# Two-layer graph network on one Trainium2 core: the first weight load in two parts, and the rounding of the first folded weight on two engines

## What is computed

```
# layer 0, seen as 2 batches of 4096 nodes in the shapes, computed per graph
q, k = split(x @ Wqk); v = x @ Wv
w    = (1/16) * mask * rowsum(q * (adj @ (k * mask)))
x1   = layernorm(x + softmax(w over the nodes) * v)
# layer 1
query, key, value = x1 @ Wq.T + bq, x1 @ Wk.T + bk, x1 @ Wv.T + bv
weight = adj * exp(query @ key.T);  weight /= rowsum(weight)
out  = layernorm(x1 + weight @ value)
```

## Time and profile before

| what | value |
|---|---|
| median of 3 runs | 291.27 us (290.82 to 291.36) |
| the profiled execution's own time | 291.13 us |
| its span | 289.1 us |
| outside the span | 2.0 us |
| PE busy | 281.0 us (97%) |
| DVE busy | 249.3 us (86%) |
| ACT busy | 248.9 us (86%) |
| POOL busy | 217.4 us (75%) |
| chain that ended last, PE's share | 92% |

### The profile page before, as it was taken

How to read it: one execution, slowest core, us unless ns; L and a number is a source line. 1 busy time by engine, 2 the same in 40 slices (tenths; PEclk the granted TensorE clock), 3 DMA queues, 4 the chain that set the end, 5 groups by cost and what they waited for, 6 DMA issues and landing times.

```text
span 289.1 us, 7132 instructions
## 1 busy us (share of the span) xinstructions
PE 281.0 (97%) x1956; PEld 261.7 (91%) x1956; DVE 249.3 (86%) x838; ACT 248.9 (86%) x625; POOL 217.4 (75%) x270
## 2 busy tenths in 40 slices
PE   8999999999999999999999999999999999999991
PEld 7878999999999999999999999999999999999990
DVE  1477999999899999998999998999999989999775
ACT  3455789999999999999999999999999999998863
POOL 1556888788897888789887888978887898877332
PEclk9999999999999999999999999999999999999997
DMA  6931232332344324234432333433233343310112
GB/s 225 344 105 37 91 94 93 94 124 83 124 127 127 98 84 127 84 116 127 127 94 89 126 90 110 127 127 104 90 115 95 104 127 127 91 50 29 52 39 110
DMA packets 19166, 31.27 MB, mean 108 GB/s; under 512 B 2128, under 2 KB 6608, under 8 KB 19152
## 3 DMA queue, kind: packets, MB, share of 16 engines
q1 hardware_dynamic: 19152, 31.11, 34.3%
HBM read 22.71 MB, written 8.39 MB: 108 GB/s over the span
## 4 chain that ended last, share of the span: by engine, by line
PE 92%; DVE 3%; DMA 2%; issue 1%; ACT 0%; POOL 0%; SPq 0%; POOLq 0%; DVEq 0%; ACTq 0%
PE ps L924 25%; PE ps L925 25%; PE ps L926 25%; PE ps L1030 9%; PE ps L1007 5%; DMA p<-params 2%; PE ps L947 1%; PE ps L1163 1%; PE ps L1035 1%; PE ps L986 1%; DVE stats L642 0%; PE ps L1170 0%; DVE x_sum L661 0%; DVE x L680 0%; DVE agg L636 0%
## 5 line engine op out<-in xcount | busy, mean ns | idle before, releaser
L924 PE MATMUL ps<-w_hi,xt_hi 128*128 128x512 f32 x124 | 49.1, 396 | 0.0
L925 PE MATMUL ps<-w_lo,xt_hi 128*128 128x512 f32 x124 | 48.6, 392 | 0.0
L926 PE MATMUL ps<-w_hi,xt_lo 128*128 128x512 f32 x124 | 48.5, 391 | 0.0
L377 POOL TENSOR_TENSOR edge_lo<-edge,edge_hi 128x256 fp32r<-128x256 f32 x29 | 21.5, 741 | 32.6 <-ACT edge_hi L558 32.6
L310 POOL TENSOR_TENSOR x1b<-x,bv_all 128x512 f32<-128x512 f32 x31 | 39.9, 1289 | 3.0 <-DVE x L865 2.1
L364 POOL TENSOR_TENSOR xt_lo<-xt_raw,xt_hi 128x512 fp32r<-128x512 f32 x31 | 39.7, 1281 | 1.8 <-ACT xt_hi L448 1.8
L388 POOL TENSOR_TENSOR rstd<-var_eps,minus_half 128x4 f32<-128x4 f32 x31 | 31.6, 1019 | 9.3 <-DVE var_eps L835 9.2
L466 ACT ACTIVATE x<-x_sum,shift,rstd 128x256 f32<-128x256 f32 x60 | 32.7, 593 | 4.3 <-POOL shift L391 4.3
L371 POOL TENSOR_TENSOR x_lo<-x_raw,x_hi 128x512 fp32r<-128x512 f32 x28 | 36.2, 1294 | 0.0
L924 PE MATMUL ps<-wv_hi,x1t_hi 128*128 128x258 f32 x124 | 35.7, 288 | 0.0
L926 PE MATMUL ps<-wv_hi,x1t_lo 128*128 128x258 f32 x124 | 35.2, 284 | 0.0
(11 more groups left out here) (171 smaller groups left out, 909.9 us busy)
## 6 DMA issues: line engine op xcount, KB each, us to landing
xt_raw<-xt_pairs SPq DMA_DIRECT2D x32, 256.0 KB, 2.7
x_raw<-x_pairs SPq DMA_DIRECT2D x32, 256.0 KB, 2.7
out_pairs<-x SPq DMA_DIRECT2D x31, 256.0 KB, 2.0
adjt<-adjt_pairs SPq DMA_DIRECT2D x32, 129.0 KB, 2.1
p<-params SPq DMA_DIRECT2D x1, 770.0 KB, 6.7
p<-params SPq DMA_DIRECT2D x1, 512.0 KB, 3.8
p<-params SPq DMA_DIRECT2D x1, 256.0 KB, 4.8
out_pairs<-x SPq DMA_DIRECT2D x2, 128.0 KB, 1.8
```

The source lines that it names most:

```text
L924: nc.tensor.matmul(out, s_hi, m_hi, start=first, stop=False)
L925: nc.tensor.matmul(out, s_hi, m_lo, start=False, stop=False)
L926: return nc.tensor.matmul(out, s_lo, m_hi, start=False, stop=last)
```

## The change

It does four things.

1. The load of `wqkT` becomes two loads of 256 KB, one for each half k of the sum (tiles k and 2+k: two pieces of 1 KB in each partition where before there was one of 4 KB), each with a semaphore of its own.
2. The first product runs with k outside and m inside: the two products of k = 0 after the first load, the two of k = 1 after the second. Half m = 0 is complete after the third product, half m = 1 after the fourth.
3. M0's half 0 is rounded by VectorE, at the head of its prologue ahead of the remainder of `xt`; half 1 is rounded by ScalarE, ahead of the value weights.
4. ScalarE rounds the two halves of the value weights one after the other, behind it.

```diff
-            sp.dma_start(p0[:, 0:4 * DIM], params0[:, 0:4 * DIM]).then_inc(wqk_loaded, 16)
+            wqk = params0[:, 0:4 * DIM].rearrange("p (t a) -> p t a", t=4)
+            for k in range(HALVES):
+                sp.dma_start(wqkT[:, k::HALVES, :], wqk[:, k::HALVES, :]).then_inc(wqk_loaded[k], 16)
             load_xt(0, 0)
...
             split_xt(0, 0)
+            act.wait_ge(m0_done, 2)
+            nc.scalar.activation(w0_hi[:, 1, 0:DIM], m0_ps[:, 1, :], ACT.Copy, scale=ATT_SCALE).then_inc(m0_hi_done[1], 1)
             act.wait_ge(wv0_loaded, 16)
             for m in range(HALVES):
                 nc.scalar.copy(w0_hi[:, m, DIM:2 * DIM], wv0[:, m, :]).then_inc(wv0_hi_done, 1)
-                act.wait_ge(m0_done, m + 1)
-                nc.scalar.activation(w0_hi[:, m, 0:DIM], m0_ps[:, m, :], ACT.Copy, scale=ATT_SCALE).then_inc(m0_hi_done, 1)
...
             nc.vector.memset(stats[:, :, :, :], 1.0).then_inc(stats_cleared, 1)
+            dve.wait_ge(m0_done, 1)
+            nc.vector.tensor_scalar(w0_hi[:, 0, 0:DIM], m0_ps[:, 0, :], ATT_SCALE, None, ALU.mult).then_inc(m0_hi_done[0], 1)
             dve.wait_ge(xt_hi_done, 1)
...
             def low_m0(m):
-                dve.wait_ge(m0_hi_done, m + 1)
+                dve.wait_ge(m0_hi_done[m], 1)
...
-            pe.wait_ge(wqk_loaded, 16)
-            for m in range(HALVES):
-                for k in range(HALVES):
+            for k in range(HALVES):
+                pe.wait_ge(wqk_loaded[k], 16)
+                for m in range(HALVES):
                     mm = nc.tensor.matmul(m0_ps[:, m, :], wqkT[:, k, m * 128:(m + 1) * 128], wqkT[:, 2 + k, :],
                                           start=(k == 0), stop=(k == HALVES - 1))
-                mm.then_inc(m0_done, 1)
+                    if k == HALVES - 1:
+                        mm.then_inc(m0_done, 1)
             pe.wait_ge(first_xt_lo_done, 1)
             for k in range(HALVES):
                 pe.wait_ge(wv0_hi_done, k + 1)
-                pe.wait_ge(m0_hi_done, k + 1)
+                pe.wait_ge(m0_hi_done[k], 1)
```

More of the change, by code:

```diff
@@ L143, in build @@
         bias_ps = ps[:, 0, 0:HALVES + 1]
-        wqk_loaded, wv0_loaded, params1_loaded, bv_loaded = sem("wqk_loaded"), sem("wv0_loaded"), sem("params1_loaded"), sem("bv_loaded")
+        wqk_loaded = sems("wqk_loaded", HALVES)
+        wv0_loaded, params1_loaded, bv_loaded = sem("wv0_loaded"), sem("params1_loaded"), sem("bv_loaded")
         x_loaded, adj_loaded, xt_loaded = sems("x_loaded", 4), sems("adj_loaded", 4), sems("xt_loaded", 2)
@@ L153, in build @@
         m0_done, at_done, bias_done = sem("m0_done"), sem("at_done"), sem("bias_done")
-        m0_hi_done, m0_lo_done, wv0_hi_done, wv0_lo_done = sem("m0_hi_done"), sem("m0_lo_done"), sem("wv0_hi_done"), sem("wv0_lo_done")
+        m0_hi_done, m0_lo_done, wv0_hi_done, wv0_lo_done = sems("m0_hi_done", HALVES), sem("m0_lo_done"), sem("wv0_hi_done"), sem("wv0_lo_done")
         wv1_hi_done, wv1_lo_done, at_hi_done, at_lo_done = sem("wv1_hi_done"), sem("wv1_lo_done"), sem("at_hi_done"), sem("at_lo_done")
```

## The result

The changed kernel takes 291.63 us (median of 13 runs, 291.05 to 292.27), the kernel before on the same chip 291.06 us (13 runs). The ratio is 1.0019 with a 95% interval of 1.0011 to 1.0027: 0.3 to 0.8 us slower, a loss clear of zero whose middle is still within 0.2%. The forecast was 291.5, +0.3.

A forecast was written before the change was run, and what follows sets the result against it. TensorE bounds the kernel (92% of the chain), so the first projection's start counts: 7.59 instead of 7.29, by ScalarE 7.57 and VectorE 7.54 to 7.60. +0.3 us on the 291.27 median gives 291.57; forecast 291.5 us, range 291.0 to 292.0.

The forecast's parts named there:

- within 0.2%: Total time: the change counts as no change, 0.2% being about 0.58 us; chance 0.84.
- The mechanism named: ScalarE's prologue: casts stand behind a rounding that waits for the whole product until 6.69; path 0.28 us longer; chance 0.77.
- VectorE's path: VectorE's prologue: remainder of xt ends at 7.40 to 7.46 behind the new rounding, TensorE starts 7.54 to 7.60, tying with ScalarE.
- Rival A: First projection: product ends before the value weights land, start 7.00, 0.29 us earlier, total 290.9 us; chance 0.06.
- rival C: TensorE before the projection: clock falls in the 0.9 us hole, loses about 2 us, total 293.5; chance 0.05.
- Start of the projection: First projection on TensorE: starts at 7.59 instead of 7.29, +0.3 us.
- The product's end: First product on TensorE: complete at 6.69, that is 6.79 less the 0.1 us gained.
- The 0.1 us gain at the first pass: First product's first pass: weights there earlier save 0.1 us, bounds 0 and 0.12.
- VectorE's rounding: Head of VectorE's prologue: rounding M0's half 0 from PSUM starts at 6.29 and takes 0.42 us, bounds 0.40 and 0.48.
- The loads behind: Loads after wqkT: issued about 0.48 us later, landings slip 0 to 0.5 us, costing nothing.
- Rival B: Loads in pieces: second part of wqkT or value weights late, projection +1.0 us, total 292.4; chance 0.12.
- An earlier or later start should reach the end one for one: From the first projection to the kernel's end: any shift of its start, forecast +0.3 us, moves the end equally.

The follow-up runs named there:

- e2: The changed kernel with the one load and the product loop of the kernel before, so the roundings alone; 291.73 us, ratio 1.0014 to 1.0036.
- e4: The changed kernel measured again without an edit, giving its second profile; 291.69 us, ratio to the kernel before 1.0014 to 1.0033.
- e9: The changed kernel with six warm-up products instead of eight; 291.67 us, ratio to the kernel before 1.0005 to 1.0023.
- e1: The kernel before with only the change's two loads and product loop, ScalarE and VectorE as before; 291.55 us, ratio 1.0011 to 1.0028.
- e6: The kernel before with its first VectorE memset in two halves, one VectorE instruction more; 290.96 us, ratio 0.9987 to 1.0009.
- e12: The kernel before measured again without an edit; 290.94 us, ratio 0.9983 to 1.0002.

## Why the prediction was right, and where it wasn't

**The sign, the place and "within 0.2%" held; the size was about half of the measured.** The forecast of +0.3 us stands against +0.57 (0.3 to 0.8). The mechanism named is real: the rounding that waits for the whole product was put in front of the casts (e2 shows it alone). VectorE's path ties with it, as forecast, but for another reason: not the new rounding in front of the remainder of `xt`, but `xt` itself, rounded only at 6.84 and in e4 at 7.4. The early half buys nothing while the warm-up holds TensorE until 4.57. Rival A (faster) didn't occur; the clock didn't fall in the longer hole (rival C): the projection's products follow one another by 0.23 us, here and in e9, where TensorE had stood for 1.34 us.

**Start of the projection, term by term.** Predicted 7.59, seen 7.75, and 8.21 in the second profile.
- *The product's end.* Taken 6.69, measured 6.95 and 7.22. The 0.1 us gain at the first pass was real: the second pass starts 0.43 us behind the first in all four kernels with two loads that start at about 4.6, against 0.55 to 0.58 in five of those with one load (0.45 in e2, whose load had landed at 4.35). But the moment of the clock's rise was taken from one execution. Before, the path ran over the landing and felt little of it; the change put the product on the path.
- *VectorE's rounding.* Taken 0.42, measured 0.42. It starts at 6.55, not 6.29, with the later product.
- *The loads behind.* "The landings may slip by 0 to 0.5 us": the value weights slipped 0.45 in the profile after, within the bound, and 1.05 in e4. `xt` slipped 1.1 to 1.7, beyond it. This is the step that failed: the late landings cost as much as the roundings by themselves (e1), and the prediction put them at nothing, with `xt_hi` ready by 6.25 at the latest, 0.46 us before VectorE would turn to it. The allowance covered the later issue and not the longer way from issue to landing (4.4 to 5.0 us instead of 3.9). Rival B had the right worry, and put it at the wrong place: the second part landed at 4.25 and cost nothing, the load behind it did.

The second pass of the change's product, from a window of TensorE's timeline between 5.22 and 5.4 us:

```profile
5.00 0.63 PE L1159 MATMUL ps<-p 128*128 128x256 f32 x1
```

**"An earlier or later start should reach the end one for one"** holds (span less start, above), but the change also moved VectorE's instructions by one place and got 0.2 to 0.3 us back at 26 us. Nothing in the trace before marked that pause as removable. It hid much of the loss in the one profile. That the forecast came this close is in part luck: the prediction missed a loss (the landings, the later clock) and a gain (the pause), and without the gain the time would be about 291.9, close to the edge of its range of 291.0 to 292.0.

**The sizes together.** With the roundings and load of before, three executions (before, e6, e12) started at 7.29, 7.22 and 6.74, mean 7.08; the changed kernel's two at 7.75 and 8.21, mean 7.98. The difference of 0.90, less the 0.2 to 0.3 of the pause, is 0.6 to 0.7, against 0.57 and 0.71 measured. That is few executions on each side; it shows that the terms are of the right size, no more.

## What to carry to other kernels

In front of a wait for several things, moving one instruction earlier on an in-order queue only helps if what it waits for is never later than what the instructions behind it wait for; put the one with the latest and most variable releaser last. Splitting a load delayed the loads behind it here by more than their later issue, and one piece that lands early is worth nothing while something else holds the engine that wants it. A path of a few tenths of a microsecond at a kernel's start should be read from several profiles, since landings and TensorE's clock move it by as much.

## What the runs showed of the hardware

- The same eight passes on TensorE took 1.99 to 3.18 us from one execution to the next, with the engine busy from 1.00 us in each; the passes are 0.43 us apart until the clock goes to the upper level and 0.22 after it, and that moment ranged from within the warm-up to 7.2 us.
- Landings of the same load in the same place varied by up to 0.7 us (value weights at 5.9 to 6.6 with one load of 512 KB in 4 KB pieces in front).
- One 512 KB load replaced by two of 256 KB delayed the next load by 0.6 to 0.8 us in 2 KB pieces and 1.1 to 1.7 us in 1 KB pieces, of which 0.5 to 0.6 us are its later issue; one load in 1 KB pieces hardly delayed it (0.15 us, within the spread).
- A pause of 0.29 us on VectorE came and went with the number of instructions ahead of it in its program, in all fourteen profiles; it was worth about 0.2 us of span, and a packet of instructions is loaded 0.7 us behind it where it stands, 0.8 to 0.9 us ahead of that place where it doesn't.
